# Two-layer attention and recurrence on one core: another order for the first loads of a kernel, and an early square root

## What is computed

```python
ln_out = layernorm(hidden_states, ln1_s, ln1_b)      # (x - m) * rsqrt(v + eps) * s + b
qkv = ln_out @ w_qkv + b_qkv                         # w_qkv is 512 x 1536: query, key, value side by side
q, k, v = jnp.split(qkv, 3, axis=-1)
scores = einsum(q, k) / sqrt(HD); scores = scores * mask - 10000.0 * (1.0 - mask)
probs = softmax(scores)                              # 16 heads of 32 channels
```

## Time and profile before

| | us |
|---|---|
| median of 3 timed runs | 2168.57 |
| lowest and highest of them | 2165.27, 2168.81 |
| the profiled execution, its own time | 2155.11 |
| its span, first to last instruction | 2153.4 |

### The profile page before, as it was taken

How to read it: one execution, slowest core, us unless ns; L and a number is a source line. 1 busy time by engine, 2 the same in 40 slices (tenths; PEclk the granted TensorE clock), 3 DMA queues, 4 the chain that set the end, 5 groups by cost and what they waited for, 6 DMA issues and landing times.

```text
span 2153.4 us, 28651 instructions
## 1 busy us (share of the span) xinstructions
PE 1940.0 (90%) x11012; PEld 1334.3 (62%) x11012; DVE 1437.3 (67%) x2431; ACT 867.1 (40%) x2024; POOL 523.9 (24%) x245
## 2 busy tenths in 40 slices
PE   5789999999999997999998999999999997885456
PEld 4566666666666664676775767757667656563233
DVE  3366667666666542122778787878878878999942
ACT  2466666666666743222312423414224213130221
POOL 1233334333343321020302202204104023130100
PEclk9799999999999998999999999999999998897687
DMA  7000010000001113544538437446365453443221
GB/s 207 25 1 25 11 35 21 16 25 11 26 14 71 40 64 98 203 139 153 188 113 271 150 125 253 148 147 219 115 191 191 137 197 108 156 137 119 90 78 49
DMA packets 155215, 234.90 MB, mean 109 GB/s; under 512 B 24152, under 2 KB 72024, under 8 KB 155080
## 3 DMA queue, kind: packets, MB, share of 16 engines
q1 hardware_dynamic: 138184, 216.28, 30.3%
q10 hardware_dynamic: 16896, 16.80, 2.3%
HBM read 191.09 MB, written 41.96 MB: 108 GB/s over the span
## 4 chain that ended last, share of the span: by engine, by line
PE 42%; DVE 7%; DMA 3%; ACT 2%; issue 2%; POOL 2%; SPq 1%; POOLq 0%; DVEq 0%; ACTq 0%
PE b_f_bank L1747 9%; PE b_a_bank L1770 9%; PE b_f_bank L1737 7%; PE b_c_bank L1780 6%; PE b_a_bank L1789 4%; DVE b_ring L1982 3%; PE b_c_bank L1770 3%; DMA b_o<-b_o_all 2%; PE b_y_bank L1809 2%; DVE b_ring L1971 1%; PE b_c_bank L1789 1%; PE b_f_bank L1897 1%; POOL b_mixed L1656 1%; DVE b_ring L1989 1%; DMA k_w_early<-in_w_dram 1%
## 5 line engine op out<-in xcount | busy, mean ns | idle before, releaser
L401 POOL TENSOR_TENSOR a_prob<-a_prob,a_rowinv 128x1024 f32<-128x1024 f32 x128 | 242.2, 1893 | 507.8 <-DVE a_rowinv L854 507.8
L1982 DVE TENSOR_TENSOR_SCAN b_ring<-b_ws,b_ring 128x1028 f32<-128x1028 f32 x128 | 354.0, 2806 | 6.1 <-ACT b_ring L2194 3.2
L1086 ACT ACTIVATE a_prob<-a_score,a_low 128x256 f32<-128x256 f32 x512 | 253.6, 497 | 226.5 <-DVE a_low L846 226.5
L1656 POOL TENSOR_TENSOR b_mixed<-b_mixed,b_xaT 128x1024 f32<-128x1024 f32 x40 | 119.9, 2998 | 606.6 <-DVE b_mixed L1999 606.5
L1747 PE MATMUL b_f_bank<-k_w_early 128*128 128x512 f32 x448 | 204.1, 603 | 12.3 <-DMA k_w_early<-in_w_dram 8.1
L1737 PE MATMUL b_f_bank<-k_hT_early,k_w_early 128*128 128x256 f32 x896 | 205.0, 385 | 6.5 <-ACT b_xaT L2174 5.7
L846 DVE CUSTOM_DVE_ANT_0 a_score<-a_score,a_fill 128x256 f32<-128x256 f32 x512 | 196.6, 447 | 4.8 <-DVE a_score L833 0.3
L1737 PEld LDWEIGHTS b_f_bank<-k_hT_early,k_w_early 128*128 128x128 f32 x896 | 169.3, 192 | 36.0 <-issue 14.0
L833 DVE SCALAR_TENSOR_TENSOR a_score<-a_S,a_mask 128x1024 f32<-128x1024 f32 x128 | 150.7, 1219 | 48.2 <-PE a_S L595 48.2
L1770 PE MATMUL b_a_bank<-b_mixed,b_shared 128*128 128x256 f32 x768 | 172.7, 382 | 4.4 <-POOL b_mixed L1656 3.2
L826 DVE TENSOR_SCALAR a_ctxT<-a_O,a_vec 128x256 f32<-128x256 f32 x64 | 31.0, 484 | 208.7 <-PE a_O L625 208.7
(11 more groups left out here) (162 smaller groups left out, 3053.1 us busy)
## 6 DMA issues: line engine op xcount, KB each, us to landing
k_w_early<-in_w_dram SPq DMA_DIRECT2D x64, 1024.0 KB, 5.3
b_vs<-b_v_all SPq DMA_DIRECT2D x32, 512.0 KB, 6.1
b_shared<-in_Wv_dram SPq DMA_DIRECT2D x8, 1024.0 KB, 5.5
b_shared<-in_Wk_dram SPq DMA_DIRECT2D x8, 1024.0 KB, 6.0
b_shared<-in_Wg_dram SPq DMA_DIRECT2D x8, 1024.0 KB, 7.5
b_shared<-in_Wo_dram SPq DMA_DIRECT2D x8, 1024.0 KB, 10.3
b_shared<-in_Wfv_dram SPq DMA_DIRECT2D x8, 1024.0 KB, 6.6
b_shared<-in_Wfk_dram SPq DMA_DIRECT2D x8, 1024.0 KB, 5.6
```

Of the source, the lines that this page charges most:

```text
L401: nc.gpsimd.tensor_tensor(two, two, inv.to_broadcast([P, 2 * TT, SEQ]), ALU.mult)\
L1086: last = nc.scalar.activation(prob[:, slot, a * SEQ:(a + 1) * SEQ], score[:, j, a * SEQ:(a + 1) * SEQ], ACT.Exp, bias=low[:, head, a:a + 1 ...
L1656: nc.gpsimd.tensor_tensor(mixed[:, f % 2, :, :], mixed[:, f % 2, :, :], xaT[:, :, 1:SEQ + 1], ALU.add)\
L1982: last = nc.vector.tensor_tensor_scan(x_, flat(ws[:, :, :]), x_, 0.0, ALU.mult, ALU.add)
```

## The change

Lines of the diff, whole:

```diff
+        warm = sb("warm", P, 1)
...
-        w_qkv_in = sem("w_qkv_in")
+        w_qkv_in = [sem(f"w_{name}1_in") for name in "qkv"]
...
+            def load_w_qkv(i):
+                sp.dma_start(w_qkv[:, :, i * DM:(i + 1) * DM],
+                             T["w_qkv"].rearrange("(c p) n -> p c n", p=P)[:, :, i * DM:(i + 1) * DM])\
+                    .then_inc(w_qkv_in[i], 16)
...
             load_x(0)
             with nc.allow_non_contiguous_dma(reason="channel vectors, once"):
+                load_w_qkv(0)
                 for name, i in vi.items():
                     sp.dma_start(vec[:, i, :], T[name].rearrange("(c p) -> p c", p=P)).then_inc(vectors_in, 16)
-            sp.dma_start(w_qkv[:, :, :], T["w_qkv"].rearrange("(c p) n -> p c n", p=P)).then_inc(w_qkv_in, 16)
             sp.dma_start(mask[:, 0, :].rearrange("p (a k) -> p a k", a=TT),
                          T["mask_self"].rearrange("(a p) k -> p a k", p=P)).then_inc(self_mask_in, 16)
+            load_w_qkv(1)
+            load_w_qkv(2)
             load_enc(0)
...
             first.hidden_self(0)
-            pe.wait_ge(w_qkv_in, 16)
+            pe.wait_ge(w_qkv_in[0], 16)
             first.self_q(0)
+            pe.wait_ge(w_qkv_in[1], 16)
             first.self_k(0)
             scores((0, 0, 0))
             first.self_q(1)
             first.self_k(1)
+            pe.wait_ge(w_qkv_in[2], 16)
             for k in range(TT):
                 first.self_v(k)
...
         def _(act):
-            act.wait_ge(vectors_in, 16 * N_VECTOR_DMAS)
             act.wait_ge(consts_made, 2)
+            nc.scalar.activation(warm[:, :], eps_col[:, :], ACT.Sqrt, bias=eps_col[:, :])
...
             root(0, "next")
+            act.wait_ge(vectors_in, 16 * N_VECTOR_DMAS)
             hidden_self(0)
```

## The result

The changed kernel takes 2159.58 us (median of 14 runs), the kernel before 2168.51 us (14 runs of the same comparison). The ratio is 0.9968, with a 95% interval from 0.9953 to 0.9983, so the change brings 3.7 to 10.2 us, 6.9 at the middle. The medians lie further apart, 8.9 us; the mean times, without one slow execution of the kernel before (2213.22 us), lie 7.0 us apart, and the text goes by the ratio. Timed once more against other runs of the kernel before, it came out at 0.9975 (0.9960 to 0.9990).

A forecast was written before the change was run, and what follows sets the result against it. The prediction took the prologue, where TensorE stands still until w_qkv lands, as the bound. Early root 0, q0's start -3.7, q0's pace 0, later loads 0 took 2168.57 to 2164.9 us, range 2160.5 to 2170.0.

The forecast's parts named there:

- So the weights end last: Kernel before, ahead of q0: w_qkv lands at 17.7 us, 4.1 us after ScalarE's activations of h end at 13.64.
- the vectors are second: Kernel before, ahead of q0: behind the weights, the last vector is the next bound, releasing the root at 8.90 us.
- The vectors' landing: Prologue, SyncE's queue: the tenth vector lands at 12.0 us because issues are held; bounds 9.4 to 12.6.
- q0's start: TensorE's prologue: q0 starts at 14.0 us in place of 17.71, a term of -3.7 us.
- q0's pace: q0's sixteen instructions on TensorE keep their length of 5.23 us: term 0, ends -1.7 to +1.7 us.
- Later loads and the two new waits: Behind q0: mask, key part, value part and later loads arrive covered, TensorE's two new waits already met; 0 us.
- The signs that were named: Profile after: query part by about 7.2, q0 at 14.0, v0 some 3.7 us earlier, first block shorter by as much.
- The sum against the profiled execution: Whole kernel: the profiled execution's 2155.11 us less 3.7 gives 2151.4 us.
- B: Prologue: the vectors are not held, land at 9.4, q0 at 11.4, -6.3 us: 2162.3 us; chance 0.15.
- C: Behind the prologue, 46 to 82 us: the gain is used up there, 0 us: 2168.6 us; chance 0.13.
- D: From 82 to 134 us: TensorE's low clock lasts into this stretch, costing up to 13.5 us: 2178.4 us; chance 0.08.
- E: From 46 to 82 us: half of TensorE's low clock goes, -7.7 us in all: 2160.9 us; chance 0.06.

The follow-up runs named there:

- root_only: Kernel before with only the early root and the vectors' wait moved behind the real root, w_qkv still one load behind the vectors; ratio 0.9997.
- loads_only: Changed kernel with ScalarE's program of the kernel before: new order of loads, no early root, vectors awaited ahead of the root; ratio 0.9989.
- act_queue: Changed kernel with the query part's load issued first of all by ScalarE on its own queue, in place of SyncE; ratio 0.9978.
- pe_fill: Changed kernel with 32 unread identity transposes on TensorE ahead of those of h and 36 between them and q0; ratio 0.9983.
- changed_again: The changed kernel as it is, timed and profiled once more; ratio 0.9975.
- names_only: Kernel before with only the one-column tile and two further semaphores allocated, neither used; ratio 1.0004.
- late_hidden: Changed kernel with fourteen small unread ScalarE activations between the wait for the vectors and the layer norm's activations, to hold back q0; ratio 0.9987.
- vec_first: Changed kernel with the query part issued behind all ten vectors; ratio 0.9961.
- best_order: ln_fill with b_q1 added to the early vectors and the other seven vectors issued behind the key part; 2153.34 us, ratio 0.9930.
- ln_fill: ln_first with unread identity transposes on TensorE, 32 ahead of those of h and 12 behind them; ratio 0.9972.
- ln_first: Changed kernel with ln1_s and ln1_b issued ahead of the query part on their own semaphore, the other eight vectors behind it; ratio 0.9976.
- vec_first_again: Changed kernel with the query part issued behind all ten vectors, timed a second time; ratio 0.9978.

## Why the prediction was right, and where it was not

The time, 2159.58 us, is inside the range (2160.5 to 2170.0) only in the sense of the ratio: 0.9968 of the 2168.57 us that the prediction started from is 2161.6 us. The median itself lies 0.9 us under the lower end. The likeliest case was a gain of 3.7 us, just inside what is no change; the interval of the measured gain begins there and its middle is at 6.9 us, on the other side. I had given 0.40 to that side and 0.50 to mine. The mechanism held in its steps as far as q0; the size of the whole gain was forecast too small, and why is open (below).

*What the weights and h are worth.* "So the weights end last" and "the vectors are second" held. root_only and loads_only are these two sentences as kernels.

*The vectors' landing* was the largest unknown and was taken at 12.0 out of 9.4 to 12.6. It was 11.9. The holds were spread over more issues than worked out (2.4 us in all over the first six, where I had the third and the fourth), the tenth was issued at 9.35 and not at 9.8, and it landed 2.5 us behind its issue and not 2.2. That 12.0 came so close is luck in part: an issue 0.45 us too late and a landing 0.3 us too quick nearly cancel. And the count of rows that gave it, 1,900 to 2,050 outstanding, is not borne out. The trace before has a row against it: the fourth vector, with x (256) and four vectors (2,048) issued, 2,304 in all, was not held. From 1.5 to 3.0 us the windows have 16, 160 and 250 GB/s, which I estimate at 0.21 MB or some 100 rows moved, so about 2,200 were out.

```profile
2.96 0.51 SPq L356 DMA_DIRECT2D a_vec<-in_b_q_dram  x1
```

act_queue then took 512 rows off the queue without shortening a hold.

*q0's start* was put at 14.0 and is 13.98. The term was -3.7 against 17.71. The two other profiles of the old order have q0 at 18.30 and 18.02, so against their mean the term is -4.1. It was mis-sized by 0.4 us because one profile stood for the kernel before.

*q0's pace* was taken at 0 and was +0.5 in the profile of the changed kernel. Over three profiles of the old order it is 5.85 us on the mean, over two of the changed kernel 5.94: 0 was right, and the cause that was guessed for the slow pace is shown by pe_fill. The two paces were not read from the earlier trace rows rightly: seven instructions in 2 us are 0.29 us each and not 0.43, since q0 in the kernel before went over from the slow to the fast pace on its way (line 496 has two instructions in the microsecond from 17.70 and six in the one from 21.70). The changed kernel's five in 2 us are the slow pace alone, 0.4.

*Later loads and the two new waits* cost nothing, as said. Fill was made at 13.02, k0 was released by q0's copy, v0 by the key's, and by the last scores the gain is still there, 3.4 us out of 4.0 (812.01 against 808.56, and 30.88 against 26.92, each on the mean of its profiles).

*The signs that were named.* The query part landed at 7.8 and not by 7.2, without effect, since q0 waited for the vectors. v0 came 3.1 us earlier (34.99 against 38.09) and not 3.7, because q0 itself took 0.5 us longer in this profile. The first block shrank by 2.8 us from the one profile to the other (VectorE's first row of the second layer is at 858.86 and 856.02), which is less than q0's 3.7; on the means of the three and the two profiles it shrank by 4.3 (861.75 and 857.42). Two single profiles could not have decided this sign.

*The sum against the profiled execution* is the step that failed. It said 2151.4 us for a profile like the one before, and the profile came out at 2159.19. The sentence that failed is "The timed runs lie 13.5 us above it for reasons that do not touch the prologue". They did not touch the prologue, but they were no constant: the rest behind the last scores took 1343.2 us in that one execution, and 1346.2 to 1359.9 in the thirteen others. The profile before was the luckiest of all. Taking the same difference off the median did no harm, since it was only the term of the prologue that went into it.

*The rivals.* B (vectors not held) was ruled out by the long issues. C (the gain is used up from 46 us on) is ruled out as far as the end of the first layer, on the means of the profiles. D and E priced the granted clock of the first iteration. The windows by stage of the changed kernel, which answer to the earlier trace rows:

```profile
46.00:82.00 36.00, 22.80 (x152) 15.94 (x150) 17.93 (x69) 23.33 (x63) 11.36 (x6) 0.63 0.10 24
82.00:134.00 52.00, 45.28 (x237) 31.00 (x238) 24.68 (x76) 20.09 (x56) 9.92 (x5) 0.90 0.08 26
```

It hardly moved from 46 to 82 us (0.63 against 0.62) and was 0.90 in place of 0.99 behind that, but changed_again has 0.94 there, and so have the old orders names_only (0.95) and root_only (0.94). So these profiles do not show that the change lowered it, and the last scores kept 3.4 of 4.0 us. The places where microseconds come and go were others, waits at the end of the first layer and the reloads of the second, which no case of mine had.

*What stays open* is the rest of the gain. The prologue accounts for 4.0 us; the ratios, 6.9 and 5.4 us, lie above it and have it inside their intervals. Of the nine other comparisons with the split loads, five gained more than their first scores are earlier (act_queue by 0.6 us, loads_only by 0.8, late_hidden by 1.9, vec_first by 3.6 and best_order by 6.1), ln_fill as much, and three less (ln_first by 0.4 us, vec_first_again by 0.5 and pe_fill by 2.5). All but best_order and the first vec_first have one to one inside their intervals. That looks for the most part like the spread of 6 to 14 runs around one to one, but whether the second layer gains a little by starting earlier can't be said from these.

## What to carry to other kernels

In a prologue that nothing overlaps with, list the inputs of the first matmul with the times at which each is ready, and change the order until they arrive together, since moving one ahead is worth only the distance to the second. Load first what is needed first, piece by piece: small vectors behind a large load come late by the whole of it and more (here 3.0 us, from 8.9 to 11.9, behind a load that moves in an estimated 2.6 us, 1.05 MB at 407 GB/s). Before a difference of a few microseconds is read off two profiles, look at a second profile of the same kernel.

## What the runs showed of the hardware that was not expected

- TensorE ran at its lower clock at the start of q0 in every kernel that let it stand still, with the granted clock recorded as 1.00: q0 took 5.2 to 6.5 us, and 3.69 us when TensorE had been kept busy.
- A wait can cost TensorE twice, and need not. 2.42 us of standing still ahead of k0 in ln_fill were followed by 5.41 us for work that takes 3.69, at a granted clock of 0.63 and 0.52. A wait of 3.17 us behind the last scores was followed by 3.69, 5.07 or 6.55 us for the same sixteen instructions, in three profiles.
- Moving a load to another engine's queue does not free the issues behind it: with the 1 MB load on ScalarE's queue, SyncE's six first vector issues took 6.4 us in place of 5.7, and x landed 2.1 us later.
- Two executions of the same program, apart from names, had spans of 2153.4 and 2172.3 us.
